# A graph-attention block with eight experts: the ninth pass over an expert's weights is folded into the eighth

## What is computed

```python
def _L0_ffn_ref(x, Wr, br, W1, b1, W2, b2):
    B, S, H, E, K = (2, 1024, 1024, 8, 2)
    logits = jnp.einsum('bsh,he->bse', x, Wr) + br
    probs = jax.nn.softmax(logits, axis=-1)
    top_p, top_i = jax.lax.top_k(probs, K)
    cw = jnp.sum(jax.nn.one_hot(top_i, E, dtype=x.dtype) * top_p[..., None], axis=-2)
    h = jax.nn.relu(jnp.einsum('bsh,ehd->bsed', x, W1) + b1)
    y = jnp.einsum('bsed,edh->bseh', h, W2) + b2
    out = jnp.einsum('bseh,bse->bsh', y, cw)
...
x = x + _L0_ffn_ref(_layernorm(x, axis=-1)[None], ...)[0]
```

## Time and profile before

| | us |
|---|---|
| median of 3 runs | 1044.91 (1044.50 to 1045.52) |
| the profiled execution's own time | 1045.54 |
| its span | 1043.8 |
| PE busy | 998.0 (96%) |
| ACT busy | 635.9 (61%) |
| DVE busy | 775.6 (74%) |

### The profile page before, as it was taken

How to read it: one execution, slowest core, us unless ns; L and a number is a source line. 1 busy time by engine, 2 the same in 40 slices (tenths; PEclk the granted TensorE clock), 3 DMA queues, 4 the chain that set the end, 5 groups by cost and what they waited for, 6 DMA issues and landing times.

```text
span 1043.8 us, 15018 instructions
## 1 busy us (share of the span) xinstructions
PE 998.0 (96%) x5191; PEld 849.0 (81%) x5227; DVE 775.6 (74%) x1078; ACT 635.9 (61%) x825; POOL 145.1 (14%) x185
## 2 busy tenths in 40 slices
PE   3999999999999999989999799999999999999998
PEld 3898899888888899978888677888887878788775
DVE  6336888776586868767754788888788878888587
ACT  4348777622321223789962567777777777777572
POOL 2002332420001002143220200000000000000013
PEclk9999999999999999989999899999999999999989
DMA  8652423255556663211106399999999999999886
GB/s 295 185 179 65 121 67 116 92 155 167 152 158 190 192 195 118 102 40 42 41 1 208 130 370 364 384 381 379 357 379 386 361 366 382 362 380 386 306 312 232
DMA packets 140508, 237.33 MB, mean 227 GB/s; under 512 B 6908, under 2 KB 48124, under 8 KB 137892
## 3 DMA queue, kind: packets, MB, share of 16 engines
q1 hardware_dynamic: 135780, 225.91, 63.1%
q0 software_dynamic: 1760, 6.37, 1.6%
q10 hardware_dynamic: 2912, 4.34, 1.1%
HBM read 206.56 MB, written 30.03 MB: 227 GB/s over the span
## 4 chain that ended last, share of the span: by engine, by line
PE 77%; DVE 9%; ACT 7%; issue 3%; DMA 3%; SPq 1%; POOL 0%; ACTq 0%; DVEq 0%; POOLq 0%
PE bank L1318 34%; PE bank L969 5%; PE bank L971 5%; PE bank L970 5%; PE bank L983 4%; PE bank L984 4%; PE bank L985 4%; PE bank L1200 2%; DVE wlo L1392 2%; DMA raw<-in_wffn 2%; PE bank L1117 2%; ACT dense L741 2%; PE bank L1044 2%; PE bank L1214 1%; ACT dense L739 1%
## 5 line engine op out<-in xcount | busy, mean ns | idle before, releaser
L1695 DVE TENSOR_TENSOR wlo<-raw,whi 128x2048 fp32r<-128x2048 f32 x72 | 164.6, 2288 | 22.8 <-ACT whi L867 22.2
L867 ACT ACTIVATE a_all<-raw 128x2048 fp32r<-128x2048 f32 x72 | 138.0, 1917 | 49.4 <-DMA raw<-in_wffn 21.2
L867 ACT ACTIVATE whi<-raw 128x2048 fp32r<-128x2048 f32 x72 | 137.8, 1914 | 35.6 <-DMA raw<-in_wffn 18.3
L1392 DVE TENSOR_TENSOR wlo<-raw,whi 128x1024 fp32r<-128x1024 f32 (+1 forms) x72 | 110.3, 1537 | 53.8 <-ACT whi L656 52.6
L656 ACT ACTIVATE whi<-raw 128x1024 fp32r<-128x1024 f32 (+1 forms) x72 | 89.0, 1242 | 95.9 <-PE bank L971 47.7
L1695 DVE TENSOR_TENSOR t_all<-raw,a_all 128x2048 fp32r<-128x2048 f32 x36 | 82.5, 2292 | 44.9 <-ACT a_all L867 44.7
L969 PE MATMUL bank<-a_all,whi 128*128 128x384 f32 x320 | 109.5, 342 | 0.2 <-DVE t_all L1467 0.2
L971 PE MATMUL bank<-a_all,wlo 128*128 128x384 f32 x320 | 107.2, 335 | 0.0
L970 PE MATMUL bank<-a_all,whi 128*128 128x384 f32 x320 | 107.1, 335 | 0.0
L1318 PE MATMUL bank<-a_all,xg 128*128 128x512 f32 x360 | 106.8, 411 | 0.0
L1318 PE MATMUL bank<-whi,t_all 128*128 128x512 f32 x288 | 100.4, 410 | 0.0
(11 more groups left out here) (276 smaller groups left out, 2092.3 us busy)
## 6 DMA issues: line engine op xcount, KB each, us to landing
raw<-in_wffn SPq DMA_DIRECT2D x144, 512.0 KB
raw<-in_wffn SPq DMA_DIRECT2D x72, 1024.0 KB
raw<-in_wall SPq DMA_DIRECT2D x28, 1024.0 KB
raw<-in_wall SPq DMA_DIRECT2D x32, 512.0 KB
yrows<-zero SPq DMA_DIRECT2D x24, 512.0 KB, 7.0
y_rows<-zero SPq DMA_DIRECT2D x8, 1024.0 KB, 8.7
dense<-yrows SPq DMA_DIRECT2D x8, 512.0 KB, 7.6
y_rows<-dense ACTq DMA_DIRECT2D x16, 256.0 KB, 5.6
```

Of the source, the lines that this page charges most:

```text
L867: act.activation(hi_ring[u % RAW], raw[:, u % RAW, :], ACT.Copy).then_inc(hi_done, 2)
L1392: dve.tensor_tensor(ring(wlo, k), part(k), ring(whi, k).bitcast(F32), ALU.subtract).then_inc(lo_done, width(k))
L1695: dve.tensor_tensor(lo_ring[u % RAW], raw[:, u % RAW, :], hi_ring[u % RAW].bitcast(F32), ALU.subtract)\
```

## The change

The last pass disappears as a pass of its own. The loop now makes the passes of seven experts, in an order in which the busiest expert (looked for among 1 to 7) has changed places with expert 7, and the last pass is that of the busiest with 192 slots: 128 as before, and 64 more whose high and low parts lie side by side in one stationary operand of 128 columns. So a unit has its 12 matmuls and 8 further ones (`extra_unit`): this stationary operand against the high and the low part of the weights. In the result the upper and lower 64 rows are added (ACT copies one half, DVE adds the other). This needs, in the last pass, a second set of hidden rows, transposes, splits, bias rows and combines.

What else moves:

- The weights' high and low rings have 3 places in the last pass and not 4, since the fourth holds the new operands; there `hi_f` of unit u+3 waits for the end of unit u.
- The ranks have to follow the exchange of the two experts. `posi` is now computed behind the busiest, in DVE's chain behind the first operand's split; further operations there make the order of the experts, the exchanged columns of `picks`, and a second matrix `back2`.
- SP reads the expert's number from `order` into a register before each pass, and issues all 16 units within the pass; the loop's turn lies between unit 15 and unit 0. The 64 further rows are loaded once, behind pass 0.
- PE's first unit of a pass waits for one half of its operand and not for both; at the front it begins when 4 of the 8 low blocks are there; `biased` is first raised at the start, so POOL's first `pick` no longer waits for PE.

The core of the diff:

```diff
+LAST = NE - 1
+XTRA = P // 2
...
+        exT = lo_ring[RAW - 1][:, 0:KT * P].rearrange("p (k c) -> p k c", k=KT)
+        ehid = hi_ring[RAW - 1].rearrange("p (k c) -> p k c", k=FT)
...
-                for u in range(PRE, UNITS):
+                for u in range(done, UNITS):
                     unit(g, u, e)
...
-            with sp.Fori(0, NE - 1) as g:
-                expert(g, g, g + 1, (g + 1) * C)
+            expert(0, 0, C)
+            sp.dma_start(ex_slot, rows[LAST * C + SLOTS:LAST * C + SLOTS + XTRA, :]).then_inc(ex_in, 16)
             sp.wait_ge(busy_ready, 4)
+            more = sp.value_load(over[0:1, 0:1], min_val=0, max_val=1)
+            def owner_of(g):
+                return sp.value_load(order[0:1, bass.ds(g, 1)], min_val=0, max_val=NE - 1)
+            with sp.Fori(1, LAST) as g:
+                expert(g, owner_of(g), (g + 1) * C)
...
-            def hi_f(g, u):
+            def hi_f(g, u, depth=RAW):
...
-                act.wait_ge(used, g * F_PIECES + LAYER_PIECES + SPLIT + 2 * (u - UP))
+                act.wait_ge(used, g * F_PIECES + LAYER_PIECES + SPLIT + 2 * (u + 1 - depth))
...
+            def last_expert(g):
+                for u in range(UNITS):
+                    if u == 0:
+                        act.wait_ge(ex_turned, 1)
+                        act.activation(exT[:, :, 0:XTRA], bank[2][:, :]..., ACT.Copy).then_inc(ex_hi, 1)
+                        act.wait_ge(g_turned, 2)
+                        act.activation(backT, ...).then_inc(back_out, 1)
+                        act.activation(backT2, ...).then_inc(back_out, 1)
...
+            def extra_unit(g, u, b, lhs, final):
+                pe.wait_ge(lo_done, g * F_PIECES + LAYER_PIECES + TURN + 2 * u + 2)
+                w_hi, w_lo = weights(u, RAW - 1)
+                for c in range(4):
+                    for n, w in enumerate((w_hi, w_lo)):
+                        last = pe.matmul(bank[b][:, :]..., lhs[:, c, :], w[:, c, :, :], start=False, ...)
+                return last
...
-            pe.wait_ge(a_ready, KT)
             for k in range(0, PAIRS, 2):
                 o, kh = k // 4, k // 2 % 2
+                pe.wait_ge(a_ready, kh + 1)
...
+                    if b == 0:
+                        pe.wait_ge(x_lo, 2 * g + 2)
+                        pe.wait_ge(ex_lo, 1)
+                        pe.wait_ge(back_out, 2)
...
-            with pe.Fori(0, NE) as g:
-                expert(g, False)
+            with pe.Fori(0, LAST) as g:
+                expert(g)
...
-            expert(more * MORE + NE, True)
+            last_expert(more * MORE + LAST)
```

More of the change, by code:

```diff
@@ L115, in build @@
         extra = sb("extra", [P, 1], I32)
-        busy = sb("busy", [P, 4, NE])
+        order = sb("order", [P, NE], I32)
+        busy = sb("busy", [P, 8, NE])
         busy_i = sb("busy_i", [P, 8], U32)
@@ L301, in build @@
         y_in = sem("y_in")
+        ex_in = sem("ex_in")
+        ex_turned = sem("ex_turned")
+        ex_hi = sem("ex_hi")
+        ex_lo = sem("ex_lo")
+        eh_copied = sem("eh_copied")
+        eh_added = sem("eh_added")
+        eh_turned = sem("eh_turned")
+        eh_hi = sem("eh_hi")
+        eh_lo = sem("eh_lo")
+        ey_full = sem("ey_full")
+        ey_copied = sem("ey_copied")
+        ey_added = sem("ey_added")
+        back_out = sem("back_out")
+        order_ready = sem("order_ready")
         got = [sem(f"got{i}") for i in range(2 * NT)]
@@ L460, in unit, with expert @@
                     sp.dma_start(dst, src[:, :, u % 4, :]).then_inc(raw_in[u % RAW], 32)
-            def expert(g, e, e_next, row):
-                for u in range(PRE, UNITS):
+            def expert(g, e, row, done=0):
+                for u in range(done, UNITS):
                     unit(g, u, e)
@@ L469, in expert @@
                         sp.dma_start(x_slot, rows[bass.ds(row, SLOTS), :]).then_inc(x_in, 16)
-                if e_next is not None:
-                    for u in range(PRE):
-                        unit(g + 1, u, e_next)
             sp.wait_ge(b_out, 32)
@@ L988, in _ @@
             pe.sem_inc(used, SPLIT)
+            pe.sem_inc(biased, 1)
             pe.wait_ge(consts, 6)
@@ L1009, in _ @@
                 if k == 0:
+                    pe.wait_ge(a_ready, 2)
                     pe.wait_ge(b_parts, 8)
@@ L1322, in combine, with turn_eh @@
+            def turn_eh(b):
+                if b >= 2:
+                    pe.wait_ge(eh_lo, b - 1)
+                pe.wait_ge(eh_added, b + 1)
+                for k in range(4):
+                    last = pe.transpose(bank[2 + b % 2][:, k * XTRA:(k + 1) * XTRA], eh_row[:, b % 2, k * P:(k + 1) * P], ident[0:XTRA, 0:XTRA])
+                last.then_inc(eh_turned, 1)
             def combine(g, i):
+                banks = [bank[(0, 1, 4, 5, 6, 7)[NT * i + t]] for t in range(NT)]
+                pe.wait_ge(ey_added, i + 1)
+                for t in range(NT):
+                    pe.matmul(banks[t][:, :], backT2[:, t, :], ey_row[:, i * 512:(i + 1) * 512], start=True, stop=False)
@@ L1324, in combine @@
                 pe.wait_ge(y_copied, 2 * g + i + 3)
                 for t in range(NT):
[L1326 to L1339 removed]
+                    pe.matmul(banks[t][:, :], backT[:, t, :], y_row[:, i * 512:(i + 1) * 512], start=False, stop=True).then_inc(comb_full, 1)
@@ L1372, in _ @@
             with pe.If(more > 0):
-                with pe.Fori(NE, NE + MORE) as g:
-                    expert(g, False)
-            expert(more * MORE + NE, True)
+                with pe.Fori(LAST, LAST + MORE) as g:
+                    expert(g)
+            last_expert(more * MORE + LAST)
         @block.vector
@@ L1829, in _ @@
             last.then_inc(g_ready, 1)
-            with dve.Fori(0, NE) as g:
-                expert(g, False)
+            link(dve.tensor_scalar(val[:, 1, :], val[:, 0, :], float(-SLOTS), None, ALU.add))
+            for t in range(NT):
+                last = dve.tensor_scalar(back2[:, t, :], slot1[:, 0:XTRA], val[:, 1, t:t + 1], w8[:, 0, t:t + 1], ALU.is_equal, ALU.mult)
+            last.then_inc(g_ready, 1)
+            with dve.Fori(0, LAST) as g:
+                expert(g)
             more = dve.value_load(over[0:1, 0:1], min_val=0, max_val=1)
             with dve.If(more > 0):
-                with dve.Fori(NE, NE + MORE) as g:
-                    expert(g, False)
-            expert(more * MORE + NE, True)
+                with dve.Fori(LAST, LAST + MORE) as g:
+                    expert(g)
+            last_expert(more * MORE + LAST)
             for i in range(NT, 2 * NT):
                 add_row(i // 2, i % 2)
+            ey_add(1)
             for o in range(2):
```

279 lines of the change are left out of this document (192 added, 87 removed).

## The result

The changed kernel took 1047.83 us (median of 12 runs, 1044.84 to 1050.93), the kernel before 1043.38 us in the same comparison (12 runs): a ratio of 1.0046, 95% interval [1.0032, 1.0061]. It is slower by 4.5 us. I had forecast 3.4 us faster. The profiled execution's span is 1048.7 us, its own time 1050.81.

The account below looks back on a forecast made before the run. PE was taken to pace the kernel, the DMA nearly full. Profiled 1045.54 - 8.2 (one pass less, longer last pass) + 5.7 (pass 0) - 0.9 (front) gave 1042.1, so a median of 1041.5 us; 8-in-10 range 1036.5 to 1047.

Parts of the forecast that it names:

- S: End of the pass ahead of the last one; ACT was forecast back at S + 8.5, PE resuming at S + 10.1.
- The head's wait: PE's stall at the head of the last pass, waiting for ACT's copies: 5.7 us against 3.97 before, +1.7.
- over 106: Sign of being wrong: the last pass, from the end of pass 6 to the span's end, forecast at 104 us.
- Passes 1 to 6 at 48.0: Loop passes between pass 0 and the last: a period of 48.0 us each; over 48.3 would show the forecast wrong.
- Pass 0: DVE's longer routing chain delays PE at unit 3 (+3.9) and the clock falls (+2.4): together +5.7 us.
- The last pass's work: Added matmuls, bias rows, turns, transposes and combines in the last pass, +36.8, and +1.3 for the further rows' turn.
- The turn in unit 8: In the last pass PE reaches the further hidden rows' turn before their sum is ready: +1.3 us, from 0 to 4.
- rival 4: PE's waits at the last pass's further-row turns make the clock fall: 1062.2 us, 1045.7 with one place; chance 0.10.
- Rival 1: Pass 0 costs little, as DVE's added operations overlap or the clock holds at unit 3: 1038.6 us; chance 0.20.
- Rival 2: Small stalls throughout the last pass and a head stall of 8 us, some 4 us more: 1045.5 us; chance 0.19.
- Rival 3: SP's loop turn costs as the skip does, losing 1.9 us in each of six passes: 1052.9 us; chance 0.06.
- The front: PE starts at the front when the first four low blocks are there: -0.9 us, between -1.2 and 0.

Follow-up runs that it names:

- the repeat: The changed kernel, unchanged, run again for a second profile and more times: 1048.04 us, ratio 1.0054 to the kernel before.
- The experiment with 25 steps: The kernel before plus 25 small unused VectorE steps at the end of the routing's chain, ahead of unit 3's low part: 1050.22 us, ratio 1.0061.
- the last two versions of the final pass first: Changed kernel, final pass in flag 0's branch, SP outputs and last DVE adds behind both branches: 1040.39 us; also routing spread, x load behind unit 11: 1038.71 us.
- the jump hidden: Changed kernel with the final pass first in flag 0's branch, and SP's outputs and DVE's last adds behind both branches: 1040.39 us, ratio 0.9966.

## Why the prediction was wrong

- **The step that failed** is SP's: "At the skip SP's sequencer stood for 4.59 us; now unit 0 of the last pass is behind that, some 3 us late, and it was ready with more to spare: 0." The delay was seen and sized (2.8 us late, forecast 3) and its cover was wrong. The ring had no unit to spare here: just ahead ACT waited 0.6 to 0.8 us for each of three units to land, where in the kernel before it waited for none of them to land. The lateness went through ACT before ACT's own skip, and the skips, each looked at alone, stood in a row, so that ACT was back at S + 14.6 and not S + 8.5. The head's wait came to 11.5 and, in the repeat, 9.3 us. The last pass with its turn took 119.0 us (mean of two) where my sum gives 73.2 + 39.8 = 113.0: 6.0 of the 7.9 us by which the median missed. From S to the end it took 110.5 us, where I had 104 and called over 106 a sign of being wrong. Of the rest, 3.3 us (mean of two) are passes 1 to 6, and pass 0 came 0.9 under its forecast. Removing all skips gives 12.3 us there in the changed kernel and 4.5 in the one before.
- **Passes 1 to 6 at 48.0**: wrong by 3.8 and, in the repeat, 2.8 us. I had read "nearly full" in the earlier trace rows and given it no price. That the loads bound these passes is shown, why they do so only in the changed kernel with PE's skip is open.
- **Pass 0**, forecast +5.7: 45.0 and 46.5 us against 40.9, so +4.1 and +5.6. The steps were right: lo_f(0, 3) at 603.55 with the front 1.5 us early, the wait 5.35, a lower clock behind it. Over the 5.6 us from the end of this wait the granted clock was 0.75 in the first profile and 0.50 in the repeat, which makes 5.6 x 0.25 = 1.4 of the 1.5 us between them:

```profile
605.98:611.58 5.60, 5.60 (x18) 4.34 (x20) 5.60 (x4) 0.60 (x1) 0.03 (x1) 0.75 0.74 226
```

```profile
601.74:607.34 5.60, 5.60 (x14) 4.11 (x14) 5.60 (x4) 0.08 (x1) 0.04 (x1) 0.50 0.69 216
```

The experiment with 25 steps confirms the mechanism.
- **The last pass's work**, 38.1: 38.0 without skips, with the two errors that cancel as said above. The turn in unit 8 waited 1.71 for 1.3; counting bias row, 12 matmuls and turn at their steps, PE is there after 3.3 us and not 3.6, which gives 1.6. The clock fell at the head (0.77 granted over 954.3 to 960.0) and nowhere behind, so rival 4 did not happen here. It was near: in the last two versions of the final pass first, the same wait of 1.7 us at unit 8 was followed by a lower clock. With the jump hidden:

```profile
987.40:993.00 5.60, 5.57 (x19) 4.48 (x21) 0.15 (x1) 2.14 (x2) 2.92 (x4) 0.70 1.01 378
```

- **The rivals.** Rival 1 fell: pass 0 cost 4.1 and 5.6 us. Rival 2 (1045.5) and rival 4 with one place (1045.7) had the nearest totals. Rival 2 had half the reason: the head's wait passed its 8 us, but there were no small stalls behind it. Rival 4's number is luck, as its mechanism did not occur. Rival 3 fell: SP's loop turn costs nothing that shows (0.20 us from release to issue), the skip ahead of unit 0 does.
- **Small slips** of the sum, 0.3 us at most: four turns at 0.3 us are 1.2 and not 1.3, and the earlier trace rows give a step of 0.23 and not 0.2285.
- **The front**, -0.9: cannot be told. The same kernel's second split of the first operand came at 592.16 in one profile and 587.91 in the other:

```profile
592.16 0.69 DVE L1895 TENSOR_TENSOR xg<-bank,xg 128x512 fp32r<-128x512 f32 x1 [1.92 <-ACT xg L919]
```

```profile
587.91 0.69 DVE L1895 TENSOR_TENSOR xg<-bank,xg 128x512 fp32r<-128x512 f32 x1 [1.93 <-ACT xg L919]
```

## What to carry to other kernels

A branch over code that is not run stopped SP for 4.7 and ACT for 5.4 us. Count which prepared work covers it on each engine, and follow a late engine through the next one's order before calling it hidden; better, put the common path first and the jump where the engine waits anyway. Whether a late load is covered is read from what the next engine waits for just ahead of it: ACT waiting for the load means no cover, ACT waiting for PE means some. Here GpSimd's scatters that began inside a 128x2048 subtraction of DVE waited it out, and so did what was queued behind them.

## What was not expected of the hardware

- Removing PE's skip, which runs once behind the loop, went with passes of the loop that were 3 us shorter in sum, in all four profiles without it (290.8 and 291.8 us to 288.0). The cause is open.
- A skip's length differs by engine: SP 4.71 us, ACT 5.41; PE, where nothing else held it, showed 2.39 to 2.51 us in four profiles, six transposes into the last pass and not at the branch, and this went with its skip.
- A scatter on POOL took 0.95 us alone. Begun inside a 128x2048 subtraction of DVE it ended 0.8 to 0.9 us behind the subtraction's end (up to 2.85 us in all); begun 0.07 us ahead of one it took 0.95.
